# Last head pair's variance by matmul, routing on capped logits, and reordered entry to the experts

## The reference

```
# mLSTM, per head:  Cn = C / (normalizer + EPS);  h = Cn @ v
mu = h.mean(-1, keepdims=True)
var = ((h - mu) ** 2).mean(-1, keepdims=True)
hn = (h - mu) * jax.lax.rsqrt(var + EPS)
hn = hn * ln_scale.reshape(1, nh, 1, dh)
...
x = x + jnp.tanh(g_xattn[0]) * mlstm(_layernorm(x), ctx, ctx, ...)
# experts, on xn = _layernorm(x):
logits = SOFTCAP * jnp.tanh(xn @ w_gate / SOFTCAP)
probs = jax.nn.softmax(logits, axis=-1)
_, idx = jax.lax.top_k(probs, TOPK)
mask = jax.nn.one_hot(idx, E, dtype=probs.dtype).sum(-2)
weights = probs * mask
for e in range(E):
    h = jax.nn.silu(x @ w1[e]) * (x @ w3[e])
    out = out + h @ w2[e] * weights[:, e:e + 1]
x = x + jnp.tanh(g_ffn[0]) * out
```

## Time and profile before

| what | value |
|---|---|
| median of 3 runs | 229.91 us (229.88 to 231.53) |
| the profiled execution | 229.46 us |
| its span, first to last instruction | 227.7 us |
| PE busy | 197.8 us, 87% |
| DVE busy | 129.8 us, 57% |
| ACT busy | 111.9 us, 49% |
| POOL busy | 88.8 us, 39% |
| mean granted PE clock | 0.956 |

### The profile page before, as it was taken

One profiled execution on the slowest core, in us unless ns is written; L12 is line 12 of the kernel. 1 busy time (PEld: TensorE's weight loads), 2 busy tenths in 40 slices (PEclk: granted clock), 3 DMA queues, 4 the chain that ended last, 5 costly groups with the idle time before them and its releaser, 6 DMA issues.

```text
span 227.7 us, 4241 instructions
## 1 busy us (share of the span) xinstructions
PE 197.8 (87%) x1331; PEld 146.4 (64%) x1332; DVE 129.8 (57%) x310; ACT 111.9 (49%) x224; POOL 88.8 (39%) x96
## 2 busy tenths in 40 slices
PE   8999899898978712769999999999999999999940
PEld 2488544444436511557888888888888888888830
DVE  6897574679899878976777852223323222222310
ACT  2478888898855795026666622233223322223210
POOL 8100343365740000510445646555444555453222
PEclk9999999999999855699999999999999999999997
DMA  3999999901011140210232233333333322334222
GB/s 117 313 367 376 371 373 374 342 24 49 0 49 46 46 153 33 62 33 1 44 53 46 46 49 46 50 55 61 57 58 42 50 46 46 46 52 62 27 23 23
DMA packets 20032, 23.41 MB, mean 103 GB/s; under 512 B 3888, under 2 KB 15152, under 8 KB 20016
## 3 DMA queue, kind: packets, MB, share of 16 engines
q1 hardware_dynamic: 13696, 16.94, 21.6%
q0 software_dynamic: 4464, 6.16, 17.2%
q10 hardware_dynamic: 1856, 0.10, 0.5%
HBM read 17.95 MB, written 5.24 MB: 102 GB/s over the span
## 4 chain that ended last, share of the span: by engine, by line
PE 74%; DVE 12%; ACT 5%; issue 4%; DMA 2%; POOL 1%; DVEq 0%; POOLq 0%; ACTq 0%
PE bank L1335 28%; PE bank L1352 17%; PE bank L1164 6%; PE bank L1061 4%; PE bank L1344 4%; PE bank L1204 3%; ACT arena L487 2%; PE bank L1317 2%; PE bank L1085 2%; DMA out_dram<-hraw,sidx 2%; PE bank L1180 2%; DVE arena L787 1%; DVE vp L968 1%; PE bank L1184 1%; PE bank L1228 1%
## 5 line engine op out<-in xcount | busy, mean ns | idle before, releaser
L447 POOL DMA_INDIRECT out_dram<-hraw,sidx x23 | 37.6, 1636 | 63.1 <-DVE hraw L1021 57.2
L1335 PE MATMUL bank<-arena_r,xn_sb_r 128*128 x184 | 57.2, 392 | 0.0
L1015 DVE TENSOR_TENSOR x_sb<-x_sb,bank 128x512 f32<-128x512 f32 x23 | 15.8, 688 | 57.5 <-ACT x_sb L637 57.5
L1352 PE MATMUL bank<-w_sb,xn_sb 128*128 x184 | 43.6, 380 | 0.8 <-ACT xn_sb L641 0.8
L1335 PEld LDWEIGHTS bank<-arena_r,xn_sb_r 128*128 128x128 f32 x184 | 34.6, 188 | 7.1
L1335 PE MATMUL bank<-w_sb_r,xn_sb_r 128*128 x92 | 38.2, 415 | 0.8 <-issue 0.6
L637 ACT ACTIVATE x_sb<-bank 128x512 f32<-128x512 f32 x23 | 13.7, 598 | 49.5 <-PE bank L1335 49.5
L1352 PEld LDWEIGHTS bank<-w_sb,xn_sb 128*128 128x128 f32 x184 | 33.2, 190 | 4.6 <-issue 1.0
L408 POOL TENSOR_SCALAR_AFFINE_SELECT arena<-arena 128x1024 f32<-128x1024 f32 x16 | 17.7, 1104 | 36.6 <-ACT arena L517 36.6
L641 ACT ACTIVATE xn_sb<-bank 128x512 f32<-128x512 f32 x23 | 13.7, 598 | 25.8 <-PE bank L1344 25.8
L787 DVE TENSOR_TENSOR arena<-bank,arena 128x1024 f32<-128x1024 f32 x16 | 19.6, 1222 | 7.0 <-POOL arena L408 6.8
(11 more groups left out here) (206 smaller groups left out, 257.8 us busy)
## 6 DMA issues: line engine op xcount, KB each, us to landing
w_sb<-in_L_ffn_w_dram SPq DMA_DIRECT2D x24, 512.0 KB, 9.3
x_sb<-in_x_dram SPq DMA_DIRECT2D x2, 512.0 KB, 6.7
arena<-in_ctx_dram SPq DMA_DIRECT2D x2, 512.0 KB, 9.3
out_dram<-x_sb SPq DMA_DIRECT2D x8, 128.0 KB, 1.8
xnorm_scratch<-xn_sb SPq DMA_DIRECT2D x8, 128.0 KB, 1.7
out_dram<-hraw,sidx POOLq DMA_INDIRECT x23, 3.8
cvT<-xnorm_scratch,gidx POOLq DMA_INDIRECT x12
hraw<-xnorm_scratch,gidx POOLq DMA_INDIRECT x11, 2.9
```

Source lines behind the costliest of these rows:

```text
L447: nc.gpsimd.indirect_dma_start(out=out[:, :], out_offset=bass.IndirectOffsetOnAxis(ap=sidx[:, i:i + 1], axis=0), in_=y_sb[i % 2], in_offse ...
L1335: last = nc.tensor.matmul(ps_scores[p][:, n, :], a, w, start=(k == 0 and j == 0), stop=(k == KC - 1 and j == 2))
L1352: last = nc.tensor.matmul(ps_tr[:, 0:H], hT_sb[p][:, k * P:(k + 1) * P], w2_sb[:, bass.ds(e * W2 + k * H, H)], start=(k == 0), stop=(k == ...
```

## The change

The last two sequences' heads: `turn_cv` uses, in the place of transposes, f32 matmuls with `to_rows`, a matrix that turns and scales by `lns` (and drops the empty columns: 68 columns in the place of 128). ACT squares `cvT` itself (`square_last`), and eight matmuls with the 0/1 matrix `in_head` (4 columns each) sum the squares of each head (`spread_last`). DVE's sum over heads and the product by `lns` are gone for this pair. The routing looks for the two largest among the capped logits and not among their exponentials; the exponentials are taken beside it. Thirteen one-hot matrices are made by DVE, in two instructions, and three by ACT. Of DVE's work ahead of the first tile, one `lower_weights` moves behind the expert numbers, and the output rows and the weights' selectors move behind the first `lower_x`; `split(1)` moves ahead of `slot_weights`. On PE the `weight_table` moves from before the first `gate_up` to after the second `turn_x`, the warm-ups change.

```diff
+        to_rows = sb("to_rows", [P, 4, 4, DH + 1])
+        in_head = sb("in_head", [P, 4])
...
+        SOME = (0, 8, NS - LATE_OH)
...
+            def square_last(i):
+                act.wait_ge(s_ots, B - 1 + i)
+                nc.scalar.activation(sqT[:, i, :], cvT[:], ACT.Square).then_inc(s_sqT, 1)
...
+                if b >= B - 2:
+                    square_last(b - B + 2)
...
-            square_heads(NG - 1)
...
+            act.wait_ge(s_th, 1)
             nc.scalar.activation(ex[:], lt[:], ACT.Exp, scale=SOFTCAP).then_inc(s_exl, 1)
...
+            act.wait_ge(s_top, 2)
+            nc.scalar.activation(wtop[:], r8[:, 0:TOPK, :], ACT.Exp, scale=SOFTCAP).then_inc(s_exl, 1)
             nc.scalar.preload_act_table_set("silu_and_others")
+            act.wait_ge(s_dump, 16)
+            act.wait_ge(s_slf, 1)
+            for n in range(LATE_OH):
+                follow(nc.scalar.activation(slotd[n % 2], iota_r[:], ACT.Abs, scale=-1.0, bias=slotf[:, n:n + 1]))
+                nc.scalar.activation(oh_r[:, NS - LATE_OH + n, :], slotd[n % 2], ACT.Relu, scale=-1.0,
+                                     bias=one_c[:, 0:1]).then_inc(s_ohl, 1)
...
+                    dve.wait_ge(s_par2, 2)
+                    rows = ident.rearrange("p (j v) -> p j v", v=VW)
+                    nc.vector.tensor_reduce(in_head[:], rows[:, :, 0:DH], AX_X, ALU.add).then_inc(s_scl, 1)
+                    nc.vector.tensor_tensor(to_rows[:, :, :, 0:DH],
+                                            lns.rearrange("p (g j d) -> p g j d", g=4, d=DH),
...
-            spread_heads(g)
+            dve.wait_ge(s_spr, 1)
+            nc.vector.scalar_tensor_tensor(out=rs[:, 0, :], in0=ps_scores[0][:, 0, 0:NH2], scalar=1.0 / DH,
+                                           in1=s16[:, 2, :], op0=ALU.mult, op1=ALU.add).then_inc(s_var, 1)
             stats_x2(g - 1)
+            finish(g)
             aggregate_x2(g - 1)
...
-            finish(g)
-            link(nc.vector.tensor_tensor(hflat, hflat, per_head(rs[:, 1, :]), ALU.mult))
+            link(nc.vector.tensor_tensor(hflat, raw_heads(g), per_head(rs[:, 1, :]), ALU.mult))
...
-            lower_weights(0, 1)
 
 
             be = lambda t: t.unsqueeze(2).to_broadcast([P, B, E])
             rev = iota_e[:, :].unsqueeze(1).to_broadcast([P, B, E])
             dve.wait_ge(s_const, 11)
-            dve.wait_ge(s_exl, 1)
-            src = ex
+            dve.wait_ge(s_th, 1)
+            src = lt
...
+            nc.vector.tensor_copy(slotf[:], sloti[:, 1, NS - LATE_OH:]).then_inc(s_slf, 1)
...
+            lower_weights(0, 1)
             lower_weights(0, 3)
...
             lower_x(0, 0)
+            token_slots()
+            select_weights()
+            split(1)
             slot_weights()
-            split(1)
             hidden(0, 0)
...
+                        last = nc.tensor.matmul(ps_h[:, g * 4 * (DH + 1):(g + 1) * 4 * (DH + 1)], part,
+                                                to_rows[:, g].rearrange("p j v -> p (j v)"), start=True, stop=True)
...
+                    for g in range(4):
+                        last = nc.tensor.matmul(ps_scores[0][:, 0, i * NH + 4 * g:i * NH + 4 * g + 4],
+                                                sqT[:, i, g * P:(g + 1) * P], in_head[:], start=True, stop=True)
...
+            spread_last()
             turn_x2(1)
             warm_up(4)
             logits(1)
...
             turn_x2(3)
+            warm_up(2)
             logits(3)
...
             last.then_inc(s_tab, 1)
+            warm_up(8)
...
-            warm_up(4)
-            warm_up_r(8, 2 * P)
-            warm_up_r(8, P)
             turn_x(0, s_xg[0], 16, 0)
-            weight_table()
             gate_up(0, 0, expert_of(0), 0)
             turn_x(1, s_xg[1], 16, 1, 1)
+            weight_table()
             turn_h(0, 0, False)
```

More of the change, by code:

```diff
@@ L173, in bass_gated_mlstm_moe_kernel @@
         etf = sb("etf", [P, NT])
+        slotf = sb("slotf", [P, LATE_OH])
+        wtop = sb("wtop", [P, TOPK, B])
         tab = sb("tab", [P, 5, NT])
@@ L264, in bass_gated_mlstm_moe_kernel @@
         s_sq = sem("heads_squared")
+        s_scl = sem("head_scales_spread")
+        s_sqT = sem("last_heads_squared")
+        s_spr = sem("last_spreads_done")
         s_dm = sem("decay_masked")
@@ L282, in bass_gated_mlstm_moe_kernel @@
         s_lg = sem("logits_done")
-        s_exl = sem("router_exp_done")
+        s_th = sem("capped_logits_done")
+        s_top = sem("top_logits_found")
+        s_exl = sem("router_exps_done")
+        s_slf = sem("late_slots_copied")
+        s_ohl = sem("late_slot_selectors_done")
         s_mask = sem("mask_done")
@@ L622, in _ @@
             act.wait_ge(s_lt, 1)
-            follow(nc.scalar.activation(lt.rearrange("p b e -> p (b e)"), lt.rearrange("p b e -> p (b e)"), ACT.Tanh,
-                                        scale=1.0 / SOFTCAP))
+            nc.scalar.activation(lt.rearrange("p b e -> p (b e)"), lt.rearrange("p b e -> p (b e)"), ACT.Tanh,
+                                 scale=1.0 / SOFTCAP).then_inc(s_th, 1)
+            act.wait_ge(s_th, 1)
             nc.scalar.activation(ex[:], lt[:], ACT.Exp, scale=SOFTCAP).then_inc(s_exl, 1)
@@ L868, in _ @@
                     nc.vector.tensor_scalar(lns[:], lns[:], tg[:, 0:1], None, ALU.mult).then_inc(s_par2, 1)
+                    dve.wait_ge(s_par2, 2)
[3 more added lines that the diff above has]
+                                            lns.rearrange("p (g j d) -> p g j d", g=4, d=DH),
+                                            rows[:, :, 0:DH].unsqueeze(1).to_broadcast([P, 4, 4, DH]),
+                                            ALU.mult).then_inc(s_scl, 1)
+                    nc.vector.tensor_copy(to_rows[:, :, :, DH:], rows[:, :, DH:DH + 1].unsqueeze(1).to_broadcast(
+                        [P, 4, 4, 1])).then_inc(s_scl, 1)
                     dve.wait_ge(s_fl, 2)
@@ L965, in _ @@
                                     ALU.mult).then_inc(s_sel, 1)
-            for q in range(4):
-                n4 = slice(q * NS // 4, (q + 1) * NS // 4)
-                nc.vector.tensor_tensor(oh_r[:, n4], iota_r[:, :].unsqueeze(1).to_broadcast([P, NS // 4, P]),
-                                        sloti[:, 1, n4].unsqueeze(2).to_broadcast([P, NS // 4, P]),
+            for q in range(2):
+                some = slice(*SOME[q:q + 2])
+                m = SOME[q + 1] - SOME[q]
+                nc.vector.tensor_tensor(oh_r[:, some], iota_r[:, :].unsqueeze(1).to_broadcast([P, m, P]),
+                                        sloti[:, 1, some].unsqueeze(2).to_broadcast([P, m, P]),
                                         ALU.is_equal).then_inc(s_sel, 1)
@@ L1061, in warm_up @@
                     nc.tensor.matmul(ps_ht[:, :], ones_b[:], ones_b[:, :].unsqueeze(1).to_broadcast([P, 4, P]),
-                                     start=True, stop=True)
-            def warm_up_r(n, w):
-                pe.wait_ge(s_wl, 3)
-                for j in range(n):
-                    nc.tensor.matmul(ps_ht[:, 0:w], arena_r[:, j * P:(j + 1) * P], w13_r[:, 0:w],
                                      start=True, stop=True)
@@ L1211, in turn_cv, with spread_last @@
                     pe.wait_ge(s_hst, b)
+                if b == B - 2:
+                    pe.wait_ge(s_scl, 3)
                 for g in range(4):
-                    last = nc.tensor.transpose(ps_h[:, g * P:(g + 1) * P], cvT[:, g * P:(g + 1) * P], ident[:])
-                last.then_inc(s_ho, 1)
+                    part = cvT[:, g * P:(g + 1) * P]
+                    if b < B - 2:
+                        last = nc.tensor.transpose(ps_h[:, g * P:(g + 1) * P], part, ident[:])
+                    else:
+                        last = nc.tensor.matmul(ps_h[:, g * 4 * (DH + 1):(g + 1) * 4 * (DH + 1)], part,
+                                                to_rows[:, g].rearrange("p j v -> p (j v)"), start=True, stop=True)
+                last.then_inc(s_ho, 1)
+            def spread_last():
+                for i in range(2):
+                    pe.wait_ge(s_sqT, i + 1)
+                    if i == 0:
+                        pe.wait_ge(s_cm, 2 * B)
+                    for g in range(4):
+                        last = nc.tensor.matmul(ps_scores[0][:, 0, i * NH + 4 * g:i * NH + 4 * g + 4],
+                                                sqT[:, i, g * P:(g + 1) * P], in_head[:], start=True, stop=True)
+                last.then_inc(s_spr, 1)
             def turn_x2(g):
```

42 lines of the change are left out of this document (25 added, 17 removed).

## The result

| | before | after |
|---|---|---|
| median | 230.05 us (229.52 to 231.53, 22 runs) | 233.22 us (230.83 to 235.69, 22 runs) |
| the profiled execution | 229.46 us | 231.51 us |
| its span | 227.7 us | 229.8 us |
| PE, DVE, ACT, POOL busy | 197.8, 129.8, 111.9, 88.8 us | 202.5, 128.7, 114.6, 89.5 us |
| mean granted PE clock | 0.956 | 0.942 |

The ratio of after to before is 1.011, with an interval from 1.0085 to 1.0135. Predicted were 228.4 us and a range up to 230.5, so the kernel is 4.8 us above the forecast and outside the range. "Slower by over 1%" had been given a chance of 0.04.

A forecast was written before the change was run, and what follows sets the result against it. Between heads and experts no engine is full: one chain sets `gate_up(1)`, after which PE never waits. +0.52 at Tanh, -0.72, -0.24 and -1.04 sum to -1.48 us: 228.4 us, range 227.2 to 230.5.

The forecast's parts named there:

- The end of the heads: Last heads to Tanh: new matmuls at 0.12 us a record, last logits at full clock in 1.06; Tanh 0.52 later.
- rival A: PE's clock falls in the new gap between first two tiles' `gate_up`; net 0 to +0.2, up to 230.1; chance 0.22.
- B: Heads cost more: at 0.2 us a record the new matmuls take 1.9 us longer, all reaching Tanh; 230.3; chance 0.12.
- the ring: Named after the prediction: PE turns a pair's x, ACT copies it, PE makes its logits, then the next pair.
- +0.85, +0.12, then replaced by the table load to +0.52 at Tanh: Delays in us: +0.85 at the addition to `x_sb`, +0.12 after the logits, +0.52 at Tanh, set by ACT's table load.
- Tanh to top 2: Routing: DVE's top 2 needs only Tanh, not the exponentials, so this stretch shortens by 0.72 us.
- top 2 to `gidx`: Routing's one-hot matrices, in two DVE instructions and three on ACT, bring `gidx` 0.24 us nearer to the top 2.
- a stall of 0.37 that stays: Unexplained 0.37 us wait before DVE's top 2; if it stays, top 2 comes +0.17 in all, not -0.20.
- The entry: Start of experts: DVE bounds from `lower_x(0)` to the hidden product, 5.62 us; `gate_up(1)` gains 1.04 against `gidx`, 1.48 in all.
- C: DVE stalls behind POOL early, making the third `c_mult` later; about +0.6 to +1.1, 229.0 to 229.5; chance 0.06.
- D: More gain at the heads, as with quicker weight loads for 4 columns; -0.5 to -0.9 more, 227.5 to 227.9; chance 0.12.
- E: ACT's table switch before Tanh drains as the skill's page says; 1.4 us later, 229.8; chance 0.02.

The follow-up runs named there:

- rest_only: After with the old end of the heads put back, new routing and entry kept; 229.22 us, ratio 0.9973 to before.
- heads_only: Before with only the new end of the heads, routing and entry as before; 232.81 us, ratio 1.0039.
- heads_late: `heads_only` with `spread_last` moved behind `turn_x2(1)` on PE; 233.42 us, ratio 1.0134.
- heads_nowarm: `heads_only` without the seven warm-up matmuls among the logits; 233.18 us, ratio 1.0141.
- after_full: After with three warm-ups ahead of each half of `spread_last`, four in a free PSUM bank, three ahead of first `gate_up`, six ahead of first `turn_h`; 229.45 us.
- rest_fuller: `rest_only` with warm-ups added: six before first `turn_h`, three before last turning of x, three before first `gate_up`, four in a free PSUM bank; 227.32 us.
- entry_only: Before with only the new entry to the experts, the same moves on DVE and PE; 230.43 us, ratio 0.9982.
- after_warm: After with two warm-up matmuls ahead of each half of `spread_last`; 233.00 us, ratio 1.0009.
- heads_wide: `heads_only` with 64 columns in the place of 4 in each matmul of `spread_last`; 231.44 us, ratio 1.0036.

## Why the prediction was wrong

**The step that failed.** It is in "The end of the heads": the last logits "at full clock, 1.06", and with them all that PE does from 73 us on. The argument for it was that `warm_up(3)` ends later and `warm_up(2)` stands ahead. That looked at the warm-ups and not at what was put before them: from 70.12 to 73.27 PE in after does nothing but the 68-column matmuls, the 4-column ones and four transposes, and the clock falls as `warm_up(4)` begins. The prediction had the pattern in hand: in rival A it noted that before's clock fell after PE "had had nothing but short matmuls and transposes". It asked that question of the new gap at 98 us and not of these 3.1 us, where before has 0.9 (70.09 to 71.00). With old heads, too, a profile shows the clock falling at 70.5 (`rest_only`), but back by 73.9; in after, `heads_only`, `heads_late` and `heads_nowarm` it stayed at half past the last logits. Under "slower" it allowed only for "A and B together or the fall of the clock over a longer stretch".

**Why a lower clock cost so much here.** The sum took the delay of `turn_x2(1)` (2.24 us in after: 72.80 for 70.56) as hidden behind the addition to `x_sb`, with 0.85 left. That cover held while a round of the ring took 2.2 us and was gone at 3.5. The term "+0.85, +0.12, then replaced by the table load to +0.52 at Tanh" measured +3.81 at Tanh; at the full clock its parts come out right by the estimate from `after_full`. The sum also has the end of `lt` 0.27 behind the end of the logits where the earlier trace rows give 0.34, a slip of 0.07 that the table load would have hidden.

**Term by term, in after.**

| term | forecast | measured |
|---|---|---|
| one record of the new f32 matmuls | 0.12 | 1.90 / 16 = 0.12 |
| variance on DVE | 73.0 | 73.05 |
| Exp of `guess_heads(3)` | 74.91 | 74.74 |
| addition to `x_sb` | 76.84, +0.85 | 76.69, +0.70 |
| `lt`, end | 80.37, +0.10 | 84.07, +3.80 |
| Tanh | 80.82, +0.52 | 84.11, +3.81 |
| Tanh to top 2 | -0.72 | -0.29 |
| top 2 to `gidx` | -0.24 | -0.31 |
| `gidx` to `gate_up(0)` | 4.86 | 4.99 |
| `gidx` to `gate_up(1)` | -1.04 | -0.98 |
| all | -1.48 | +2.23 |

**Tanh to top 2.** The prediction put the other end beside its value: "a stall of 0.37 that stays". In after it stayed: DVE starts 0.46 us after Tanh's end. In `rest_fuller` it is gone: 0.10 after the end, and from Tanh's start to the top 2 are 0.36 us in the place of before's 1.01, that is -0.65 where -0.72 was forecast; 0.18 us of idle time one instruction later takes part of it back. The step was right but for the stall (see the last section).

**The entry** was read rightly for after, whose clock was up before `gate_up(0)`: DVE is the bound from `lower_x(0)` to the hidden product (98.61 to 104.22, 5.61 us, forecast 5.62), and `gate_up(1)` stands 1.65 behind it (forecast 1.62).

**The rivals.** A is real: a fall in the gap stands in the profiles of `entry_only` and `after_warm`. It is not in after's (the clock is full from 97.4 on), so it is not the cause of the 2.05 us there; whether it is part of after's slower executions is open. B is right in that the heads cost more (3.3 us at Tanh above the forecast), but by the clock and not by a record's price. C did not happen: the third `c_mult` starts at 32.13, and the new instructions ahead of it took 0.22, 0.42 and 0.18. They ran between two masks of POOL (31.14 to 32.11), so the contention behind this rival wasn't put to the test. D did not happen: 4 columns cost as much as 8. E: in `after_full` Tanh starts 0.01 us after the end of the table load (80.57 + 1.28 = 81.85). The Trainium skill, "ScalarE: Activation LUTs", section "What ACT_TABLE_LOAD costs", would have a drain of about 1.38 us there; the trace disagrees with it, and the measurement decides.

**What stays open.** What makes the clock fall near 70 us wasn't settled, and what keeps it from coming back with the new heads neither. The 4-column matmuls aren't needed for a fall (`heads_late`), nor are the 68-column ones (`rest_only`); `heads_wide` did not tell. Why the fall comes at 71.4 in one execution and at 73.5 in another of the same instructions is open as well. Of after itself, one execution was profiled; that its slower ones are like the profile of `heads_only` is argued from their clocks (down to 0.921 against 0.924), not seen. And `after_full` added warm-ups at the entry as well as at the heads, so its narrow spread belongs to both together.

## What to carry to other kernels

When work moves to PE "because it is idle there", ask what the sum becomes if PE's clock is at half behind it: here the delay of 2.2 us was hidden at the full clock and passed to the end at half. So ask of every slack that hides a delay whether it is still there at half clock: a ring that has room at 2.2 us a round becomes the bound at 3.5. Warm-up matmuls in the waits of the queue took the scatter out and gave 1.9 us, 0.8%, from `rest_only` (229.22) to `rest_fuller` (227.32); the rest of its 1.2% over before is the routing and the entry. Two at a time, at the heads alone (`after_warm`), left the scatter as it was.
